# Forming mixed expert weights in 64x128 tiles instead of 96x32, with the weight split on GpSimd and another order of the opening

## What is computed

```python
x = jnp.transpose(hidden_states, (1, 0, 2))
h = jax.nn.relu(jnp.einsum('bsh,oh->bso', x, gW1) + gb1)
gate = jnp.einsum('bsh,eh->bse', h, gW2) + gb2
g = gate.mean(axis=1)
W1 = jnp.einsum('be,eoi->boi', g, eW1)
b1 = g @ eb1
W2 = jnp.einsum('be,eoi->boi', g, eW2)
b2 = g @ eb2
y = jax.nn.relu(jnp.einsum('bsi,boi->bso', x, W1) + b1[:, None, :])
y = jnp.einsum('bsi,boi->bso', y, W2) + b2[:, None, :]
```

## Time and profile before

| | us |
|---|---|
| median of 3 runs | 1060.94 |
| lowest and highest run | 1047.39, 1061.96 |
| profiled execution | 1049.67 |
| span in its trace (first to last instruction) | 1047.9 |
| mean granted clock of TensorE, share of full speed | 0.928 |

### The profile page before, as it was taken

One profiled execution on the slowest core, in us unless ns is written; L12 is line 12 of the kernel. 1 busy time (PEld: TensorE's weight loads), 2 busy tenths in 40 slices (PEclk: granted clock), 3 DMA queues, 4 the chain that ended last, 5 costly groups with the idle time before them and its releaser, 6 DMA issues.

```text
span 1047.9 us, 43971 instructions
## 1 busy us (share of the span) xinstructions
PE 816.8 (78%) x19206; PEld 694.7 (66%) x19206; DVE 556.5 (53%) x838; ACT 525.0 (50%) x809; POOL 301.4 (29%) x445
## 2 busy tenths in 40 slices
PE   3787999989875548787787888787878787878782
PEld 3656777777763426676676777676767676767682
DVE  6756667667653125455544465355445454554451
ACT  3446667667653114555554555455446345555450
POOL 7434455545423201141141141132132131231110
PEclk9889999999999557999999899899999899999997
DMA  6558667666714656787777688567858767886533
GB/s 171 133 154 217 153 174 167 164 168 154 180 25 100 135 72 123 143 174 135 141 165 143 129 157 166 113 131 148 171 114 153 153 134 140 151 170 133 104 64 72
DMA packets 94663, 146.50 MB, mean 140 GB/s; under 512 B 18858, under 2 KB 72218, under 8 KB 88226
## 3 DMA queue, kind: packets, MB, share of 16 engines
q1 hardware_dynamic: 94498, 144.02, 65.8%
HBM read 102.78 MB, written 41.03 MB: 137 GB/s over the span
## 4 chain that ended last, share of the span: by engine, by line
PE 52%; DMA 16%; issue 14%; SPq 7%; DVE 6%; POOL 2%; ACT 1%; DVEq 0%; ACTq 0%
PE banks L1730 19%; PE banks L1704 19%; DMA k_stack<-k_dram 9%; DMA ring<-split_dram 3%; PE banks L313 3%; SPq L486 2%; PE banks L1547 2%; SPq L628 2%; PE banks L1389 2%; PE banks L1430 2%; PE banks L1412 2%; DMA y<-xmid_dram 1%; SPq L493 1%; DVE w_rest L1142 1%; PE banks L1751 1%
## 5 line engine op out<-in xcount | busy, mean ns | idle before, releaser
L1033 ACT ACTIVATE wb<-banks 128x896 f32<-128x896 f32 x310 | 279.1, 917 | 310.4 <-PE banks L1704 310.0
L1704 PE MATMUL banks<-spread,ring 96*32 96x224 bf16 x8192 | 343.8, 273 | 76.2 <-issue 58.8
L1704 PEld LDWEIGHTS banks<-spread,ring 96*32 96x32 bf16 x8192 | 241.3, 101 | 104.7 <-issue 78.2
L1266 DVE COPY wb<-banks 128x896 f32<-128x896 f32 x202 | 219.4, 1086 | 120.7 <-PE banks L1704 120.6
L1730 PE MATMUL banks<-wb,ht 128*32 128x128 f32 x3584 | 164.8, 284 | 31.4 <-issue 30.1
L1730 PE MATMUL banks<-wb,xt 128*32 128x128 f32 x3584 | 161.8, 283 | 23.3 <-issue 22.6
L780 POOL CAST w_split<-w_rest 128x1024 bf16<-128x1024 f32 x32 | 33.3, 1040 | 480.6 <-DVE w_rest L1142 480.6
L1730 PEld LDWEIGHTS banks<-wb,ht 128*32 128x32 f32 x3584 | 119.5, 114 | 42.6 <-issue 37.9
L1121 DVE TENSOR_REDUCE maxima<-banks 112x2 f32<-112x750 f32 x128 | 117.8, 934 | 33.1 <-PE banks L1389 30.2
L1730 PEld LDWEIGHTS banks<-wb,xt 128*32 128x32 f32 x3584 | 115.1, 114 | 30.3 <-issue 26.4
L837 ACT ACTIVATE probs<-banks 128x448 f32<-128x448 f32 x192 | 100.5, 544 | 28.1 <-PE banks L1412 26.1
(11 more groups left out here) (129 smaller groups left out, 928.8 us busy)
## 6 DMA issues: line engine op xcount, KB each, us to landing
ring<-split_dram SPq DMA_DIRECT2D x384, 128.0 KB, 4.6
split_dram<-w_split SPq DMA_DIRECT2D x32, 768.0 KB, 4.6
w_nat<-in_w SPq DMA_DIRECT2D x64, 256.0 KB, 5.7
k_dram<-k_parts SPq DMA_DIRECT2D x16, 576.0 KB, 3.8
k_stack<-k_dram SPq DMA_DIRECT2D x32, 288.0 KB
k_stack<-k_dram SPq DMA_DIRECT2D x32, 192.0 KB
c_raw<-in_ctx_t SPq DMA_DIRECT2D x16, 375.0 KB, 5.5
k_stack<-k_dram SPq DMA_DIRECT2D x32, 96.0 KB
```

The source lines that it names most:

```text
L1033: act.activation(outputs_of(n, q), formed(bank), ACT.Copy).then_inc(form_act, 1)
L1266: dve.tensor_copy(outputs_of(n, q), formed(bank))\
L1704: last = pe.matmul(banks[32 * j:32 * j + 32, form_bank(half) + r // 2, 256 * (r % 2):256 * (r % 2) + 2 * NQ], ring[0:ROWS, t // 8, P * (t ...
```

## The change

Forming: `ring` becomes [128 partitions][64 slots][128], two tiles of E x SLOTS = 8 x 8 rows (six products used, two slots zero). One tile holds one of the two row sets of before, so that a 64-row matmul with 128 weight columns and 112 moving columns gives what four 96x32 matmuls with 224 columns gave in part: a half is now 4 r x 2 t = 8 matmuls. `spread` is [128][112]. The six loads of a part write every eighth partition. Halves go in pairs (`both`) between pairs of value groups; both turns stand at a period's start.

Split: ACT only copies PSUM to `w_rest`; POOL does cast, subtraction, cast, subtraction. DVE's `rest` is gone.

Opening: `turn(2, .)` moves behind the first eight halves, the gate ahead of it, b1 and b2 products use the units' banks, and SP loads `y` before store_split(1) and (2). POOL clears `ring` once in the attention part.

```diff
-ROWS = PRODUCTS * 2 * E
+SLOTS = 8
+TILE = E * SLOTS
-        SIX, SEVEN = (1, 3, 6, 9, 11, 14), (1, 3, 5, 8, 10, 12, 14)
+        SEVEN = (1, 3, 5, 7, 9, 11, 13)
             if n == 0:
-                return q % 2 == 1
-            return q in (SEVEN if first_half(n - 1) else SIX)
+                return q in (1, 3, 6, 9, 11, 14)
+            return q % 2 == 1 if first_half(n - 1) else q in SEVEN
-        TURN_AHEAD = 3
+        TURN_AHEAD, TURN_EARLY = 3, 2
+        def opening(form, bias1, bias2, turn):
+            def both(k):
+                form(0, 2 * k)
+                form(0, 2 * k + 1)
+            both(0)
+            bias1(0)
+            bias1(1)
+            both(1)
+            bias2(0)
+            bias2(1)
+            both(2)
+            bias2(2)
+            both(3)
+            turn(TURN_EARLY, 0)
+            turn(TURN_EARLY, 1)
+            for k in range(4, 8):
+                both(k)
+                bias2(k - 1)
         def period(n, form, turn, hidden, value):
-            form(n + 1, 0)
             turn(n + TURN_AHEAD, 0)
-            form(n + 1, 1)
             turn(n + TURN_AHEAD, 1)
...
+            both(0)
+            if not hidden_before(n):
+                for k in range(1, HALVES // 2):
+                    values(2 * k - 2, 2 * k)
+                    both(k)
+                return
...
         def formed(bank):
-            return (banks[:, bank:bank + 2, :].rearrange("p a (r c) -> p (a r) c", r=2)[:, :, 0:2 * NQ]
-                    .rearrange("p r (b k) -> p b k r", k=2))
+            return banks[:, bank:bank + 2, 0:4 * NQ].rearrange("p t (r b) -> p b t r", r=4)
...
-                    for k, piece in enumerate((0, 0, 0, 1, 1, 2)):
-                        src = split_dram[m, piece].rearrange("(r s) f -> r s f", s=8)
-                        sp.dma_start(ring[2 * E * k:2 * E * k + 2 * E, 4 * part:4 * part + 4, :],
-                                     src[:, 4 * part:4 * part + 4, :]).then_inc(ring_loaded[part], 16)
+                    if m == 0:
+                        sp.wait_ge(ring_zeroed, 1)
+                    for n, piece in enumerate((0, 0, 0, 1, 1, 2)):
+                        src = split_dram[m, piece].rearrange("(e t k) f -> t e k f", e=E, t=2)
+                        sp.dma_start(ring[n:P:SLOTS, 32 * part:32 * part + 32, :].rearrange("p s i -> p (s i)"),
+                                     src[:, :, 4 * part:4 * part + 4, :]).then_inc(ring_loaded[part], 16)
-            for m in range(TURN_AHEAD):
-                load_natural(m + 1)
-                store_split(m)
-                if m == 0:
-                    load_ring(m, 0)
-                    load_ring(m, 1)
+            load_natural(1)
+            store_split(0)
+            load_ring(0, 0)
+            load_ring(0, 1)
+            load_natural(2)
...
+            store_split(1)
             load_ring(1, 0)
+            load_natural(3)
             load_ring(1, 1)
+            store_split(2)
...
+                if s.i is None and s.c == LOOP_STEP + 2 * LOOPS:
+                    queries_stored(pool, 3)
+                    pool.wait_ge(q_mm, 2 * NG)
+                    pool.memset(ring[:].rearrange("p s i -> p (s i)").bitcast(F32), 0.0).then_inc(ring_zeroed, 1)
...
             def split(m):
                 if turns_alive(m):
-                    pool.wait_ge(turn_rest, 2 * m + 2)
+                    pool.wait_ge(turn_copied, 2 * m + 2)
                     need(pool, turn_stored, 16 * m)
+                    pool.tensor_copy(w_split[:, 0], w_rest[:]).then_inc(turn_high, 1)
+                    pool.wait_ge(turn_high, m + 1)
+                    pool.tensor_tensor(w_rest[:], w_rest[:], w_split[:, 0], ALU.subtract).then_inc(turn_rest, 1)
+                    pool.wait_ge(turn_rest, m + 1)
                     pool.tensor_copy(w_split[:, 1], w_rest[:]).then_inc(turn_mid, 1)
...
-                    act.activation(w_split[:, 0, 4 * w:4 * w + 4, :].rearrange("p q i -> p (q i)"),
-                                   banks[:, turn_bank(m, w), :], ACT.Copy).then_inc(turn_high, 1)
+                    act.activation(w_rest[:, 4 * w:4 * w + 4, :].rearrange("p q i -> p (q i)"),
+                                   banks[:, turn_bank(m, w), :], ACT.Copy).then_inc(turn_copied, 1)
...
                 for r in range(4):
-                    t = 4 * q + r
-                    for j in range(4):
-                        last = pe.matmul(banks[32 * j:32 * j + 32, form_bank(half) + r // 2, 256 * (r % 2):256 * (r % 2) + 2 * NQ],
-                                         ring[0:ROWS, t // 8, P * (t % 8) + 32 * j:P * (t % 8) + 32 * j + 32],
-                                         spread[0:ROWS].rearrange("p b k -> p (b k)"), start=True, stop=True)
+                    for t in range(2):
+                        rows = slice(TILE * t, TILE * t + TILE)
+                        last = pe.matmul(banks[:, form_bank(half) + t, NQ * r:NQ * r + NQ], ring[rows, 4 * q + r, :],
+                                         spread[rows], start=True, stop=True)
                 last.then_inc(form_mm, 1)
```

More of the change, by code:

```diff
@@ L162, in build @@
         lasting = Region(start, at_keep)
-        ring = lasting.take("ring", [P, HALVES // 2, 8 * P], BF16)
+        ring = lasting.take("ring", [P, P // 2, P], BF16)
         w_nat = lasting.take("w_nat", [P, E, P], F32)
@@ L166, in build @@
         w_rest = lasting.take("w_rest", [P, 8, P], F32)
-        spread = lasting.take("spread", [P, NQ, 2], BF16)
+        spread = lasting.take("spread", [P, NQ], BF16)
         b1_t = lasting.take("b1_t", [P, OT, NQ], F32)
@@ L363, in period, with both, values @@
+        def period(n, form, turn, hidden, value):
+            def both(k):
+                form(n + 1, 2 * k)
+                form(n + 1, 2 * k + 1)
+            def values(start, end):
+                for g in range(start, end):
+                    value(n, g)
             turn(n + TURN_AHEAD, 0)
-            form(n + 1, 1)
             turn(n + TURN_AHEAD, 1)
[L366 to L382, removed]
+            both(0)
[4 more added lines that the diff above has]
+                return
@@ new lines, in period @@
+            i = ORDER[n - 1][1]
+            hidden(i, 0)
+            hidden(i, 1)
+            both(1)
+            if ORDER[n][0] == "in":
+                values(0, 2)
+                both(2)
+                values(2, 4)
+                both(3)
+                values(4, 7)
+                both(4)
+                hidden(i, 2)
+                hidden(i, 3)
+                values(7, 9)
+                both(5)
+                values(9, 11)
+                both(6)
+                values(11, GRP)
+                both(7)
+            else:
+                hidden(i, 2)
+                hidden(i, 3)
+                for k in range(2, HALVES // 2):
+                    both(k)
+                    values((0, 2, 4, 7, 9, 11)[k - 2], (2, 4, 7, 9, 11, GRP)[k - 2])
@@ L406, in first_half @@
             return ORDER[n][0] == "in" and ORDER[n][2] == 0
+        opening(lambda n, q: None, lambda k: number(("bias1", k), "act"), lambda k: number(("bias2", k), "dve"), number_turn)
         for n in range(CHUNKS):
@@ L428, in unit_taken @@
             who, count = TAKEN[v]
-            eng.wait_ge({"act": unit_act, "dve": unit_dve, "turn": turn_rest}[who], count)
+            eng.wait_ge({"act": unit_act, "dve": unit_dve, "turn": turn_copied}[who], count)
         def turn_bank(m, w):
-            return 4 + w if m < TURN_AHEAD else 6 + turn_unit(m, w) % 2
+            return 4 + w if m < TURN_EARLY else 6 + turn_unit(m, w) % 2
         def groups(u):
@@ L1055, in first_values @@
                         .then_inc(unit_act, 1)
-            for q in range(HALVES):
-                taken_by_act(0, q)
+            opening(taken_by_act, bias1, lambda k: None, turned)
             for n in range(CHUNKS):
@@ L1311, in _ @@
             dve.wait_ge(spread_mm, 1)
-            dve.tensor_copy(spread[0:ROWS].rearrange("p b k -> p (b k)"), banks[0:ROWS, 6, 0:2 * NQ]).then_inc(spread_done, 1)
-            for w in range(2):
-                rest(2, w)
-            dve.wait_ge(y_loaded, 16 * 8)
-            for q in range(HALVES):
-                taken_by_dve(0, q)
-                if q % 2 == 0 and q // 2 < GRP // 2:
-                    add_b2(q // 2)
+            dve.tensor_copy(spread[:], banks[:, 6, 0:NQ]).then_inc(spread_done, 1)
+            opening(taken_by_dve, lambda k: None, add_b2, lambda m, w: None)
             for n in range(CHUNKS):
-                period(n, taken_by_dve, rest, add_bias, add_value)
+                period(n, taken_by_dve, lambda m, w: None, add_bias, add_value)
         @block.tensor
@@ L1654, in _ @@
             gate_hidden(7)
-            for w in range(2):
-                turn(2, w)
             for n in range(2 * NG):
```

106 lines of the change are left out of this document (46 added, 60 removed).

## The result

The changed kernel takes 1455.72 us (1454.03 to 1461.02) where the kernel before takes 1058.38: a ratio of 1.379, 95% interval 1.368 to 1.390. The profiled execution is 1456.46 us, its span 1454.7. The forecast was 1470.

The account below looks back on a forecast made before the run. PE with its own gaps bounded the kernel before; afterwards ring loads on two engines would. Opening to 408, 30 chunks x 34 = 1020, last halves 8, end 27.6, outside the span 1.8: 1465, rounded up to 1470 us; range 1400 to 1600.

Parts of the forecast that it names:

- Two engines: Ring loads: the new source's outermost count of 2 confines each load to two of 16 DMA engines; chance 0.84.
- The rate: Ring loads: 26.6 GB/s an engine, 29.6 us a chunk, plus 4 for store and w_nat: period about 34 us.
- rival 3: Ring loads: two engines at the crowded 12.2 GB/s each, about 68 us a period, 2500 us; chance 0.02.
- Crowding came from 16 busy engines: DMA rate: argument against two engines running at the crowded 12.2 GB/s each.
- On the path: Periods: the two engines never run dry and PE waits for the ring, some 15 to 20 us a period.
- The opening: Before the periods: first form near 350, y landed about 371, chunk 1's second part landed at 408 us.
- The sum: Whole kernel: opening, periods, last halves, end and time outside the span add to 1465, forecast 1470 us.
- Form half: PE's eight new form matmuls: 0.20 to 0.42 us a half, hidden behind the ring.
- A change of shape: PE switching between tile shapes: 0.1 us each, 16 a period instead of 4, +1.2 us, hidden.
- The ring's zeroing: One POOL memset in the attention part: costs 0, at most about 4 us.
- The split: POOL's weight split of 6.4 us for 3.2 delays the store 3 to 4 us; hidden at 34 us a period.
- Rival 1: Ring loads spread over 8 or 16 engines, PE sets a 16.5 us period: 920 us (860 to 990); chance 0.10.

Follow-up runs that it names:

- e1: Changed kernel with weight rows laid out so each ring load's source has outermost count 16 (sixteen engines), natural load in four smaller pieces: 881.83 us, 0.841 of the kernel before.
- e4: Kernel before with only the ring loads' source read in 2 times 8 order, outermost count 2 (two engines): 1490.86 us, 1.42, run once.
- e3: e1 with each ring load's source read in 4 times 4 order, outermost count 4 (four engines): 1022.7 us, 0.974, run once.
- e8: e1 with the six loads of the ring's first half ahead of the split's store in SP's queue: 835.17 us, 0.800 of the kernel before.
- e10: e8 with the split as before (ACT copies the high part into w_split, VectorE subtracts, GpSimd does middle and low): 911.50 us, 0.863 of the kernel before.
- e11: Kernel before with each ring load writing its 16 rows to every sixth of 96 partitions, selection matrix ordered to match: 960.44 us, 0.913.
- e12: e8 with each ring load writing to 16 neighbouring partitions in place of every eighth: 940.47 us, 0.885 of the kernel before.

## Why the prediction was right

**Two engines.** Shown, by e1, e4 and the short windows (1.9 and 2.1 engines). It was read from three small q_stack loads in one window of 1.4 us. The rule that the prediction cites beside it from the Trainium skill ("DMA: Bandwidth & Descriptors", Why a DMA increments its semaphore by 16 and not by 1) agrees with the windows of e4 and e3, outermost counts 2 and 4 (2.1 and 4.2 engines), and with e1's time at 16. The share of 0.23 at 86 GB/s was forecast as 0.2 at 80 to 90.

**The rate.** The period came out at 33.17 against 34. At the 26.2 GB/s an engine of its packets the ring took 30.0 us, forecast 29.6 (26.6, read from one window of 0.2 us), which leaves 3.2 for store and natural load, forecast 4. The crowded rate of 12.2, rival 3, did not come about. "Crowding came from 16 busy engines" is half of why it was low before: e8 has sixteen engines at 18.2, and e4 writes to neighbours on two engines at full rate; it takes both, many engines and neighbouring partitions.

**On the path.** 16.7 us a period of ring waits, forecast 15 to 20; issue waits gone, as said.

**The opening.** First form 351.51, forecast 350. Then a term was off: the prediction has y landed at 371, and PE could go on with it at 383.72. It let SP issue freely; in fact the two natural loads ahead of y took 13.1 us to issue and y's eight 12.1. Chunk 1's second part was late by as much: PE has it at 421.58, forecast 408.

**The sum.** In the prediction's own form: 421.6, 30 x 33.17 = 995, 8 for the last halves, 28 for the end and 1.8 outside the span make 1454, and the profiled execution took 1456.46. So two terms were mis-sized against each other, the opening by +13.6 us and the periods by 30 x -0.83 = -25; that the forecast lies so near owes something to this.

**What was hidden, as e1 to e10 size it.** Form half 0.20 us: the lower bound of 0.20 to 0.42 was the truth. The two 64-row tiles run at once: in e1 the two matmuls of a pair start 3 to 4 ns apart, and the next pair 49 ns after. A change of shape 0.125 where 0.1 was read. The ring's zeroing: one POOL memset of 3.5 us at 267.9, bound 4. The split: nothing at 34 us a period, as argued ("form half 8 comes later still"), but part of a 53 us wait at e1's 15.68, so that argument held only under its cover. Rival 1, had the loads spread, was put at 920 us; e1 is 882: 15.68 a period for 16.5, because halves cost 0.20 and not 0.25 and the issue waits are nearly nil where I carried over 2.7 us a period from their count before, less 1.7 of ring waits that the rival did not have.

## What to carry to other kernels

Before a DMA's pattern is rearranged, look at the count of its outermost dimension: with two there on the source side this kernel took 38% longer than before, and taking it back turned the same change into a gain of 16%, of 20% with the ring's first part ahead of the store in the queue. A DMA share that falls while the time rises does not by itself mean narrow transfers: from e8 to e10 it falls from 0.72 to 0.62, all on sixteen engines, as the period grows with waits (0.72 x 14.04 / 16.50 = 0.61). Take a short window with one kind of transfer in it: there 0.12 and 0.13 were two engines, 0.26 four. When tile shapes alternate on TensorE, put like next to like: at 0.125 us a change a half and a group took 0.755 us in pairs and 0.88 singly, where the old tiles took 0.82. And when a layout changes several things at once, test each on the old kernel: here half of the gain needed only another destination for the loads (e11).

## What the runs showed of the hardware

- With sixteen engines at work it matters where a load writes. With 16 rows to 16 neighbouring partitions all transfers together moved 11.2 to 12.2 GB/s an engine, with rows to every sixth or eighth partition 18.2 to 18.6 (e12 and before; e8 and e11), and this alone was worth 11% and 9%. With two engines it made no difference that shows: the periods are 33.93 us to neighbours (e4) and 33.17 spread out. The Trainium skill has a rule that bears on it ("SBUF — State Buffer", Door 1: The DMA port swizzle): bits 2 to 4 and 6 of the partition number choose one of 16 ports. By it, worked out for each load, 16 neighbours reach 4 ports, every eighth of 128 reaches 8 and every sixth of 96 reaches 13 or 14. The two spread patterns agree with it against the packed one; that 13 ports did little better than 8 (18.6 and 18.2) no run here explains.
- SP's issue of a transfer can be held up by transfers issued before it. The median issue of a store took 8.9 us in the changed kernel and 3.0 in e4, both with ring loads on two engines, and 0.37 before and in e1. A natural load took up to 12.7 us in the changed kernel (median of the periods 1.0), but 0.44 at the median of e4's. That full queues hold SP up fits this, but was not shown.
- The granted clock went with PE's waits: 0.71 in the periods of the changed kernel, where PE is busy half the time, 0.93 in e1 and 0.99 in e8.
